# Two weights' low parts in the directed phase's second unit, a left copy ahead of the context, and the last phase's first values in the first two banks

## The chip, the cores and the metric

The kernel runs on one core of a Trainium2 chip. Its time is the device time of one execution in microseconds (us). The engines of the core that matter here are TensorE (PE, matmuls), VectorE (DVE), ScalarE (ACT) and GpSimd (POOL); SyncE (SP) issues the DMA transfers.

## The reference

128 graphs of 64 nodes with 384 features pass through four residual layers of attention kind. What is computed, cut down:

```python
h = jnp.maximum(_layernorm(x, axis=-1), 0.0)
x = x + _L0_gnn_ref(h, adj, ...)   # 12-head attention with an output projection
h = jnp.maximum(_layernorm(x, axis=-1), 0.0)
x = x + _L1_gnn_ref(h, adj, ...)   # two bilinear layers
h = jnp.maximum(_layernorm(x, axis=-1), 0.0)
x = x + _L2_gnn_ref(h, adj, ...)   # two directed layers, below
h = jnp.maximum(_layernorm(x, axis=-1), 0.0)
x = x + _L3_gnn_ref(h, adj, ...)   # 12-head attention, scores masked by adj

# a directed layer of _L2_gnn_ref
a = jax.nn.softmax(jnp.einsum('bid,bjd->bij', h, h) / temper, axis=-1)
delta = a * adjacency_matrix
attn = delta / (jnp.sum(delta, axis=-1, keepdims=True) + 1e-10)
hl, hs, hr = h @ wl.T + b_l, h @ ws.T + b_s, h @ wr.T + b_r
ctx = jnp.einsum('bij,bjd->bid', attn * upper, hl) + diag_a[..., None] * hs \
      + jnp.einsum('bij,bjd->bid', attn * lower, hr)
h = relu(layer_norm(ctx) * g + beta)
```

## The kernel before, in words

All 8192 rows are worked in 16 groups of 512 rows (four tiles of 128). The four layers are four phases of one program: l0, l1, l2 (the directed phase) and l3 (the last phase). Every engine has a stream of instructions written out by hand, in a fixed order; the streams meet only at semaphores.

An fp32 product is made of three passes: each operand is split into a high part (`w_hi`, `hT_hi`) and a low part (`w_lo`, `hT_lo`), and `split_matmul` (L58) adds high x high, high x low and low x high over three chunks of the features: nine matmuls into one of eight PSUM banks. The high part of a weight is a ScalarE copy, the low part a VectorE subtraction `raw - high` of 128x1152 elements (L2221 in the directed phase).

The directed phase has 32 units: a unit is one group in one of the two layers. Units 0 and 1 are groups 0 and 1 in layer 0; unit 2 is the first of layer 1. In a unit TensorE makes for each tile a left, a right and a self part (each one `split_matmul`), transposes the attention (L2512), weighs (context, L2567: two halves, tiles 0 and 1, then 2 and 3), passes on three transposes of the rows for the unit above (L2480) and its score products (L2501). VectorE copies each left part (L2293) and self part (L2302, L2306) out of PSUM with its bias, ScalarE each right part (L2164), to which GpSimd adds the bias (L2074). The parts share four banks, so part t+1 waits until the copy of an earlier part has been made: self part 2 waits for left copy 2 and for the contexts of tiles 0 and 1, left part 3 and right part 3 wait for self copies 0 and 1, self part 3 waits for left copy 3. VectorE makes the context (L2315), its statistics (L2323, L2327), the variance `l_c_var` (L2329); GpSimd takes the root of that (`l_c_scale`, L2079), and VectorE makes the shift `l_c_nb` (L2336) from it.

In the first unit (`below is None`), whose first parts are made in the phase's entry in other banks, VectorE's order after the variance is: left copy 2, two weights' low parts (`weights((CARRIED, CARRIED + 1))`), `passed(1)` (a low part of the rows, L2251), `l_c_nb`, left copy 3, `passed(2)`, self copy 2, self copy 3, and the third weight's low part. Those three weights are the ones of layer 1. TensorE waits for all three at the end of unit 1. SP loads the last phase's weights when all three are made.

The last phase's entry makes three query and three key products in banks 0 to 5, and the values of the first two tiles in banks 6 and 7. The scores go to banks 4 to 7, so they wait until VectorE has copied the queries (L640), ScalarE the keys (L442) and both values (L454). The later tiles' values go to banks 0 and 1.

Of the kernel before, what the change touches and what calls it, by code (L numbers as in the profile page):

```python
# [24 lines left out]
P = 128  # L25
GRAPHS, NODES, D = 128, 64, 384
# [5 lines left out]
HEADS, HD = 12, 32  # L32
# [4 lines left out]
CARRIED = 3  # L37
# [14 lines left out]
def split_matmul(nc, out, lhs, rhs, chunks=KC):  # L52

    n, last = 3 * chunks, None
    for c in range(chunks):
        for k, (a, b) in enumerate(((0, 0), (0, 1), (1, 0))):
            m = 3 * c + k
            last = nc.tensor.matmul(out, lhs[a](c), rhs[b](c), start=(m == 0), stop=(m == n - 1))  # L58
    return last
# [35 lines left out]
def attention_phase(nc, ctx, name, shared, x_in, adj_rows, x_out, biases, own_weights, next_weights):  # L95
# [112 lines left out]

    def k_sums(i, c):
        return banks[:, 2 * c + 1, :] if not proj and isinstance(i, int) and i == 0 else psW[k_bank[c]]  # L210

    def v_sums(i, t):
        return banks[:, 6 + t, :] if not proj and isinstance(i, int) and i == 0 and t < 2 else psW[v_bank[t]]

    q_bank, k_bank, v_bank = ((0, 0, 1), (1, 0, 0), (1, 1, 1, 0)) if proj else ((0, 0, 0), (1, 1, 1), (0, 1, 0, 1))

# [185 lines left out]
    def _(act):  # L402
# [46 lines left out]
        def values(i, t):  # L449
            act.wait_ge(v_done, i * TILES + t + 1)  # L450
            for g in range(2):
                for b in range(2):
                    src = v_sums(i, t)[NODES * g:NODES * (g + 1), 0:D].rearrange("p (a b d) -> p a b d", b=2, d=HD)
                    ins = nc.scalar.activation(vX[NODES * b:NODES * (b + 1), t, g, :, 0:HD], src[:, :, b, :], ACT.Copy)  # L454
            ins.then_inc(v_set, 1)

# [121 lines left out]
    def _(dve):  # L578
# [91 lines left out]
        def values(i, t):  # L670
            dve.wait_ge(v_done, i * TILES + t + 1)
            for g in range(2):
                for b in range(2):
                    part = slice(NODES * b, NODES * (b + 1))
                    src = v_sums(i, t)[NODES * g:NODES * (g + 1), 0:D].rearrange("p (a b d) -> p a b d", b=2, d=HD)
                    bias = bv[part, :].rearrange("p (a b d) -> p a b d", b=2, d=HD)[:, :, b, :]
                    ins = nc.vector.tensor_tensor(vX[part, t, g, :, 0:HD], src[:, :, b, :], bias, ALU.add)  # L677
            ins.then_inc(v_set, 1)
# [146 lines left out]
    def _(pe):  # L825
# [11 lines left out]
        def w_cols(s, cols):  # L837
            slot = s if proj else slot_of(s)
            return tuple((lambda c, w=w: w[:, slot, c, cols]) for w in (w_hi, w_lo))

        def h_cols(cols):
            return tuple((lambda c, x=x: x[:, c, cols]) for x in (hT_hi, hT_lo))
# [206 lines left out]
        if proj:  # L1049
            for t in range(TILES):  # L1050
                if t >= 2:
                    pe.wait_ge(hT_set, t - 1)
                transposes(0, t)
            pe.wait_ge(hT_set, TILES)
            pe.wait_ge(w_lo_set, Q + 1)
            queries(0, 0)
            pe.wait_ge(w_lo_set, K + 1)
            keys(0, 0)
            pe.wait_ge(q_set, 1)
            queries(0, 1)  # L1060
            pe.wait_ge(k_set, 1)
            queries(0, 2)
            pe.wait_ge(q_set, 2)
            keys(0, 1)
            pe.wait_ge(w_lo_set, n_w)
            pe.wait_ge(q_set, 3)
            values(0, 0)
            pe.wait_ge(k_set, 2)
            keys(0, 2)
            pe.wait_ge(v_set, 1)  # L1070
            values(0, 1)
            pe.wait_ge(zeroed, 2)
            wait_apart(k_set, 3)
            scores(0, 0)
            scores(0, 1)
            transposes(1, 0)
            transposes(1, 1)
            turns(pe, projected_turn)
        else:
            ended = shared["l2_ended"]  # L1080
            h_all = h_cols(slice(0, COLS))

            def first_product(bank, s, c, signal):
                split_matmul(nc, banks[:, bank, :], w_cols(s, slice(c * P, (c + 1) * P)), h_all).then_inc(signal, 1)

            def first_values(t):
                split_matmul(nc, banks[:, 6 + t, 0:D], h_cols(slice(t * P, (t + 1) * P)), w_cols(V, slice(0, D)))\
                    .then_inc(v_done, 1)

            pe.wait_ge(*ended["hT_set"])  # L1090
            pe.wait_ge(*ended["left_set"])
            pe.wait_ge(*ended["w_lo_set"])
            first_product(0, Q, 0, q_done)
            pe.wait_ge(*ended["right_read"])
            first_product(1, K, 0, k_done)
            pe.wait_ge(*ended["s_set"])
            first_product(2, Q, 1, q_done)
            pe.wait_ge(*ended["self_set"])
            first_product(3, K, 1, k_done)
            first_product(4, Q, 2, q_done)  # L1100
            pe.wait_ge(*ended["hT_hi_set"])
            first_product(5, K, 2, k_done)
            pe.wait_ge(*ended["c_set"])
            first_values(0)
            first_values(1)
            pe.wait_ge(zeroed, 2)
            pe.wait_ge(q_set, KC)
            pe.wait_ge(v_set, 2)
            wait_apart(k_set, KC)
            scores(0, 0)  # L1110
            scores(0, 1)
            turns(pe, plain_turn)
# [706 lines left out]
def directed_phase(nc, ctx, shared, x_in, adj, x_out, a, next_weights):  # L1819
# [394 lines left out]
    def _(dve):  # L2214
# [134 lines left out]
        def result(u, x):  # L2349
            if x == 0:  # L2350
                dve.wait_ge(xr_in, (u.q + 1) * 16)
            dve.wait_ge(affine_set, 2 * (u.q * TILES + x + 1))
            nc.vector.scalar_tensor_tensor(xr[:, x, :], out_rows[:, x, :], 0.0, xr[:, x, :], ALU.max, ALU.add)\
              .then_inc(y_set, 1)

        def unit(u, below, above, stats):
            carries = is_last(above)
            before = Unit(u.n - 2, u.q - 1, 1, 0) if finishes(u) else below if is_last(u) else None

            def passed(c):  # L2360
                hT_part(above.n * KC + c, above.parity, c)

            if below is not None:
                context(below, 2)
                context(below, 3)
            less_maximum(u)
            if below is not None:
                context_variance(below, 1)
            if below is None:
                left_copy(u, 0)  # L2370
                left_copy(u, 1)
            attention(u)
            if below is None:
                self_copy(u, 0)
                self_copy(u, 1)
            else:
                left_copy(u, 0)
            row_sums(u)
            if below is not None:
                context_norm(below, 1)  # L2380
                left_copy(u, 1)
            row_factors(u)
            attention_sides(u)
            if stats:
                q, g, x = to_normalise(u)
                if is_last(u):
                    dve.wait_ge(x1_in, 16)
                else:
                    dve.wait_ge(xl_in, q * 16)
                statistics(x)  # L2390
            if before is not None:
                result(before, 0)
                result(before, 1)
            if below is not None:
                self_copy(u, 0)
            row_diagonal(u)
            if stats:
                variances(g)
            passed(0)
            if below is not None:  # L2400
                self_copy(u, 1)
            if before is not None:
                result(before, 2)
                result(before, 3)
            if stats:
                shifts(q, g)
            step.catch_up()
            context(u, 0)
            context(u, 1)
            context_variance(u, 0)  # L2410
            left_copy(u, 2)
            if below is None:
                weights((CARRIED, CARRIED + 1))
            passed(1)
            context_norm(u, 0)
            if carries:
                next_weight(0)
            left_copy(u, 3)
            passed(2)
            if carries:  # L2420
                next_weight(1)
            self_copy(u, 2)
            if carries:
                next_weight(2)
            self_copy(u, 3)
            if below is None:
                weights((CARRIED + 2,))
            if is_last(u):
                context(u, 2)
                context(u, 3)  # L2430
                context_variance(u, 1)
                context_norm(u, 1)
                result(u, 0)
                result(u, 1)
                own_affine(3)
                result(u, 2)
                own_result(3)
# [329 lines left out]
```

## Time and profile before

| | us |
|---|---|
| median of three runs | 2691.43 |
| the three runs | 2688.78, 2691.43, 2691.6 |
| the profiled execution | 2689.87 |
| its span | 2688.1 |
| TensorE busy | 2649.9 (99%) |
| VectorE busy | 1775.0 (66%) |
| ScalarE busy | 1242.2 (46%) |
| GpSimd busy | 1070.2 (40%) |

The span is the time between the first and the last instruction of the profiled execution. In a timeline a bracket behind a row gives the idle time of the engine ahead of it and what ended it. The directed phase runs from about 1397 us to 2217 us of the span, and the last phase to the end.

### The profile page before, as it was taken

What the parts mean: (1) busy time and instruction counts of PE and PEld (TensorE: products, weight loads), DVE (VectorE), ACT (ScalarE), POOL (GpSimd) and SP (SyncE); (2) the same over time, 40 slices, a digit from 0 to 9 for tenths busy, and PEclk for the clock granted to TensorE, in tenths of its full rate; (3) what the DMA queues carried; (4) which work ended last, traced back from release to release, by engine and by line L of the source; (5) the groups of instructions that cost most, each with busy time, mean ns of one, the idle gap of its engine ahead of it and who ended that gap; (6) DMA issues with size and microseconds to landing.
All of it is one profiled execution on the core that took longest, in us unless ns stands there. A gap on an engine that the chain in (4) does not pass through costs nothing.

```text
span 2688.1 us, 78153 instructions
## 1 busy us (share of the span) xinstructions
PE 2649.9 (99%) x31118; PEld 2315.3 (86%) x31118; DVE 1775.0 (66%) x4024; ACT 1242.2 (46%) x2179; POOL 1070.2 (40%) x1094
## 2 busy tenths in 40 slices
PE   7999999999999999999999999999999999999998
PEld 6888888887888888888888888888888888998997
DVE  6777778775555555555577777777777785666664
ACT  4444444444453444444453433443343345655654
POOL 2433334442322322432333434434434454555454
PEclk9999999999999999999999999999999999999999
DMA  4222222225112212212221112112112122322321
GB/s 146 76 74 63 59 63 74 74 71 161 37 55 83 72 35 70 82 36 60 76 59 57 42 45 70 41 45 70 41 39 76 40 70 83 97 74 89 97 74 62
DMA packets 187155, 183.93 MB, mean 68 GB/s; under 512 B 79632, under 2 KB 186896, under 8 KB 187024
## 3 DMA queue, kind: packets, MB, share of 16 engines
q1 hardware_dynamic: 187024, 181.99, 22.1%
q8 instruction: 106, 1.74, 0.3%
q14 instruction: 25, 0.20, 0.0%
HBM read 131.61 MB, written 50.33 MB: 68 GB/s over the span
## 4 chain that ended last, share of the span: by engine, by line
PE 92%; DVE 4%; issue 2%; ACT 1%; SPq 0%; POOL 0%; DMA 0%; DVEq 0%; POOLq 0%; ACTq 0%
PE banks L58 68%; PE banks L2567 3%; PE banks L890 3%; PE banks L877 3%; PE banks L870 3%; PE banks L1750 2%; PE banks L2480 2%; PE banks L2501 2%; PE banks L1774 2%; PE banks L847 2%; PE banks L1710 1%; PE banks L899 1%; DVE l_o_rows L694 1%; DVE l_stats L598 1%; DVE l_vX L677 1%
## 5 line engine op out<-in xcount | busy, mean ns | idle before, releaser
L58 PE MATMUL banks<-w_hi,hT_hi 128*128 128x384 f32 x1152 | 401.0, 348 | 4.6 <-DVE l_left L2293 4.6
L58 PE MATMUL banks<-w_hi,hT_lo 128*128 128x384 f32 x1152 | 387.4, 336 | 0.0
L58 PE MATMUL banks<-w_lo,hT_hi 128*128 128x384 f32 x1152 | 386.5, 335 | 0.0
L58 PE MATMUL banks<-hT_hi,w_hi 128*128 128x512 f32 (+1 forms) x954 | 365.7, 383 | 1.2 <-DVE hT_lo L635 1.2
L58 PE MATMUL banks<-hT_hi,w_lo 128*128 128x512 f32 (+1 forms) x954 | 355.1, 372 | 0.0
L58 PE MATMUL banks<-hT_lo,w_hi 128*128 128x512 f32 (+1 forms) x954 | 354.5, 372 | 0.0
L1424 ACT ACTIVATE l_m<-banks 128x512 f32<-128x512 f32 x192 | 114.8, 599 | 399.6 <-PE banks L58 394.7
L336 POOL TENSOR_TENSOR l_s_d<-l_s_b,l_mx 128x768 f32<-128x768 f32 x128 | 188.8, 1475 | 206.9 <-DVE l_mx L665 191.5
L58 PE MATMUL banks<-w_hi,l_hT_hi 128*128 128x384 f32 x768 | 266.0, 346 | 0.8 <-DVE l_lin L1540 0.8
L58 PE MATMUL banks<-w_hi,l_hT_lo 128*128 128x384 f32 x768 | 258.4, 336 | 0.0
L58 PE MATMUL banks<-w_lo,l_hT_hi 128*128 128x384 f32 x768 | 258.2, 336 | 0.0
L58 PEld LDWEIGHTS banks<-w_hi,hT_hi 128*128 128x128 f32 x1152 | 217.0, 188 | 10.4 <-issue 3.8
L1349 POOL TENSOR_TENSOR l_c_root<-l_c_mv,l_half 128x2 f32<-128x2 f32 x64 | 44.7, 699 | 435.4 <-DVE l_c_mv L1557 435.4
L58 PEld LDWEIGHTS banks<-w_lo,hT_hi 128*128 128x128 f32 x1152 | 217.4, 189 | 0.7
L58 PEld LDWEIGHTS banks<-w_hi,hT_lo 128*128 128x128 f32 x1152 | 216.8, 188 | 0.0
L58 PEld LDWEIGHTS banks<-hT_hi,w_hi 128*128 128x128 f32 x954 | 180.4, 189 | 41.0 <-issue 9.6
L58 PEld LDWEIGHTS banks<-hT_hi,w_lo 128*128 128x128 f32 x954 | 180.1, 189 | 32.1
L58 PEld LDWEIGHTS banks<-hT_lo,w_hi 128*128 128x128 f32 x954 | 180.6, 189 | 26.7
L2079 POOL TENSOR_TENSOR l_c_scale<-l_c_var,l_half 128x2 f32<-128x2 f32 x64 | 48.6, 759 | 323.5 <-DVE l_c_var L2329 323.5
L459 ACT ACTIVATE l_eT<-banks 128x768 f32<-128x768 f32 x128 | 104.3, 815 | 143.7 <-PE banks L877 142.1
L58 PEld LDWEIGHTS banks<-w_hi,l_hT_hi 128*128 128x128 f32 x768 | 144.4, 188 | 4.6 <-DVE l_lin L1540 1.1
L350 POOL TENSOR_TENSOR xr<-xr,l_y_rows 128x384 f32<-128x384 f32 x60 | 62.0, 1033 | 209.1 <-ACT l_y_rows L473 209.1
(230 smaller groups left out, 6178.8 us busy)
## 6 DMA issues: line engine op xcount, KB each, us to landing
after_l<-xr SPq DMA_DIRECT2D x160, 192.0 KB, 1.9
l_xl<-after_l SPq DMA_DIRECT2D x37, 768.0 KB, 5.0
xr<-after_l SPq DMA_DIRECT2D x24, 768.0 KB, 4.6
xr<-in_x SPq DMA_DIRECT2D x64, 192.0 KB, 2.4
xr<-after_l SPq DMA_DIRECT2D x64, 192.0 KB, 2.3
out_x<-xr SPq DMA_DIRECT2D x64, 192.0 KB, 2.1
xa<-in_x SPq DMA_DIRECT2D x15, 768.0 KB, 5.2
xa<-after_l SPq DMA_DIRECT2D x11, 768.0 KB, 6.9
```

Source lines behind the costliest of these rows:

```text
L58: last = nc.tensor.matmul(out, lhs[a](c), rhs[b](c), start=(m == 0), stop=(m == n - 1))
L336: nc.gpsimd.tensor_tensor(s_d[:], s_b[:, t], mx[:, t, :].rearrange("p (h n) -> p h n", n=1).broadcast_to([P, HEADS, NODES]), ALU.subtract) ...
L350: nc.gpsimd.tensor_tensor(xr[:, t, :], xr[:, t, :], y_rows[:, t % 2, :], ALU.add).then_inc(y_set, 1)
L459: nc.scalar.activation(eT[:, t % 2].rearrange("p a n -> p (a n)"), P_all, ACT.Copy).then_inc(eT_set, 1)
L847: ins = nc.tensor.transpose(hT_sums(i, t)[:, c * P:(c + 1) * P], h[:, t, c * P:(c + 1) * P], ident[:])
L870: ins = nc.tensor.matmul(psS[NODES * g:NODES * (g + 1), r, lo + c * NODES:lo + (c + 1) * NODES], qT[head, c, nodes], kT[head, c, nodes], s ...
L877: ins = nc.tensor.transpose(P_all[:, a * P:(a + 1) * P], e_x[:, a * P:(a + 1) * P], ident[:])
L890: ins = nc.tensor.matmul(psS[NODES * g:NODES * (g + 1), r, lo:lo + HD + 1], eT[keys_b, x, a, NODES * g:NODES * (g + 1)], vX[keys_b, 2 * p ...
L1424: nc.scalar.activation(m[:, j % KC, :, 1 - j // KC, :], m_sums(i, k, j).rearrange("p (g n) -> p g n", n=NODES), ACT.Copy).then_inc(m_set, 1)
L1750: ins = nc.tensor.matmul(psU[first:first + HALF, t * P + cols.start:t * P + cols.stop], hT_whole[k % 2][:, c, t * P + first:t * P + first ...
L1774: ins = nc.tensor.matmul(psC[NODES * c:NODES * (c + 1), PAIR * p + b, 0:D + 1], delta[NODES * b:NODES * (b + 1), PAIR * p + c, :], lin[NOD ...
L2567: ins = nc.tensor.matmul(psC[NODES * c:NODES * (c + 1), odd, 0:D], dT[nodes, t, s, :], side[nodes, t, :], start=(s == 0), stop=(s == 1))
```

## The change

In the directed phase VectorE makes two of the three low parts in unit 1 instead of unit 0, one ahead of self copy 0 and one behind self copy 1. In unit 0, left copy 2 goes ahead of the contexts of tiles 0 and 1; in all other units it stays. In the last phase's entry the first two tiles' values go to banks 0 and 1, behind the first query and key copies, and the scores no longer wait for the value copies.

```diff
-    def v_sums(i, t):
-        return banks[:, 6 + t, :] if not proj and isinstance(i, int) and i == 0 and t < 2 else psW[v_bank[t]]
...
             def first_values(t):
-                split_matmul(nc, banks[:, 6 + t, 0:D], h_cols(slice(t * P, (t + 1) * P)), w_cols(V, slice(0, D)))\
+                split_matmul(nc, banks[:, t, 0:D], h_cols(slice(t * P, (t + 1) * P)), w_cols(V, slice(0, D)))\
                     .then_inc(v_done, 1)
...
-            pe.wait_ge(*ended["c_set"])
+            pe.wait_ge(q_set, 1)
             first_values(0)
+            pe.wait_ge(k_set, 1)
             first_values(1)
             pe.wait_ge(zeroed, 2)
+            pe.wait_ge(*ended["c_set"])
             pe.wait_ge(q_set, KC)
-            pe.wait_ge(v_set, 2)
             wait_apart(k_set, KC)
...
+        def is_second(u):
+
+            return isinstance(u.n, int) and u.n == 1
+
...
+            if is_second(u):
+                weights((CARRIED,))
             if below is not None:
                 self_copy(u, 0)
             row_diagonal(u)
...
                 result(before, 3)
+            if is_second(u):
+                weights((CARRIED + 1,))
             if stats:
                 shifts(q, g)
+            if below is None:
+                left_copy(u, 2)
             step.catch_up()
             context(u, 0)
             context(u, 1)
             context_variance(u, 0)
-            left_copy(u, 2)
-            if below is None:
-                weights((CARRIED, CARRIED + 1))
+            if below is not None:
+                left_copy(u, 2)
             passed(1)
```

The two readers of `v_sums` (the value copies of ScalarE and VectorE) read `psW[v_bank[t]]` instead.

## Rows read from the trace of the kernel before

**Rows 1.** The page's busy times: engine, busy us, share of the span, instructions.

```profile
PE 2649.9 (99%) x31118; PEld 2315.3 (86%) x31118; DVE 1775.0 (66%) x4024; ACT 1242.2 (46%) x2179; POOL 1070.2 (40%) x1094
```

**Rows 2.** TensorE's waits: who waited for whom, us in total, times, longest.

```profile
PE banks L847 <- ACT l_h L422: 7.8, 1, 7.8
PE banks L58 <- DVE l_left L2293: 4.6, 2, 3.5
```

**Rows 3.** TensorE's timeline, first unit: start, us, engine, line, operation [idle before].

```profile
1409.33 0.34 PE L58 MATMUL banks<-w_hi,hT_lo 128*128 128x384 f32 x1
1410.70 0.44 PE L58 MATMUL banks<-w_hi,hT_hi 128*128 128x384 f32 x1 [1.04 <-DVE l_left L2293]
```

**Rows 4.** The chain of waits, first and second unit: start, us, what.

```profile
1416.08 2.40 PE banks L58 x9
1418.48 2.45 PE banks L2567 x16
...
1433.02 1.45 PE banks L2567 x16
...
1440.18 4.68 PE banks L58 x27
```

**Rows 5.** Stretches: busy time of each engine, then TensorE's granted clock, DMA share, GB/s.

```profile
1416.00:1418.00 2.00, 1.92 (x9) 1.92 (x9) 1.00 (x2) 1.87 (x3) 0.00 (x0) 0.77 0.01 2
1418.00:1420.00 2.00, 2.00 (x14) 0.80 (x16) 1.43 (x3) 0.00 (x0) 0.00 (x0) 0.50 0.00 0
1420.00:1422.00 2.00, 2.00 (x46) 1.14 (x40) 1.97 (x3) 0.00 (x0) 0.00 (x0) 0.88 0.00 0
...
2224.00:2226.00 2.00, 0.41 (x17) 0.18 (x23) 0.00 (x0) 1.38 (x5) 0.00 (x0) 1.00 0.31 98
```

**Rows 6.** VectorE's timeline in the first unit.

```profile
1405.40 0.68 DVE L2251 TENSOR_TENSOR l_hT_lo<-hT_whole,l_hT_hi 128x512 fp32r<-128x512 f32 x1
1407.64 1.14 DVE L2315 SCALAR_TENSOR_TENSOR l_con<-l_selves,l_own,banks 128x384 f32<-128x384 f32 x2 [1.56 <-issue]
...
1410.02 0.16 DVE L2329 SCALAR_TENSOR_TENSOR l_c_var<-l_squared,l_c_mv 128x2 f32<-128x2 f32 x1
...
1410.57 3.43 DVE L2221 TENSOR_TENSOR w_lo<-w_raw,w_hi 128x1152 fp32r<-128x1152 f32 x2
1413.92 1.48 DVE L2251 TENSOR_TENSOR l_hT_lo<-hT_whole,l_hT_hi 128x512 fp32r<-128x512 f32 x1
...
1415.39 0.54 DVE L2293 TENSOR_TENSOR l_left<-banks,l_biases 128x384 f32<-128x384 f32 x1
...
1419.68 1.36 DVE L2221 TENSOR_TENSOR w_lo<-w_raw,w_hi 128x1152 fp32r<-128x1152 f32 x1
```

**Rows 7.** GpSimd's timeline in the first and second unit.

```profile
1410.26 0.71 POOL L2079 TENSOR_TENSOR l_c_scale<-l_c_var,l_half 128x2 f32<-128x2 f32 x1 [7.34 <-DVE l_c_var L2329]
1410.94 3.91 POOL L2074 TENSOR_TENSOR l_right<-l_right,l_biases 128x384 f32<-128x384 f32 x2
...
1438.78 1.07 POOL L2074 TENSOR_TENSOR l_right<-l_right,l_biases 128x384 f32<-128x384 f32 x1
```

**Rows 8.** VectorE's timeline in the second unit.

```profile
1427.40 0.56 DVE L2293 TENSOR_TENSOR l_left<-banks,l_biases 128x384 f32<-128x384 f32 x1 [0.92 <-PE banks L58]
...
1438.89 0.98 DVE L2336 SCALAR_TENSOR_TENSOR l_c_nb<-l_c_mv,l_c_scale 128x2 f32<-128x2 f32 x1
1439.79 0.55 DVE L2293 TENSOR_TENSOR l_left<-banks,l_biases 128x384 f32<-128x384 f32 x1
```

**Rows 9.** The chain of waits at the last phase's entry, ahead of the first scores.

```profile
2224.27 1.59 issue
```

**Rows 10.** ScalarE's timeline at the last phase's entry.

```profile
2221.16 0.69 ACT L442 ACTIVATE l_kT<-banks,l_bk 128x512 f32<-128x512 f32 x1 [3.00 <-PE banks L58]
2222.74 1.34 ACT L454 ACTIVATE l_vX<-banks 64x192 f32<-64x192 f32 x4 [0.90 <-PE banks L58]
2224.30 1.34 ACT L454 ACTIVATE l_vX<-banks 64x192 f32<-64x192 f32 x4 [0.22 <-PE banks L58]
```

More of the change, by code:

```diff
@@ L452, in values @@
                 for b in range(2):
-                    src = v_sums(i, t)[NODES * g:NODES * (g + 1), 0:D].rearrange("p (a b d) -> p a b d", b=2, d=HD)
+                    src = psW[v_bank[t]][NODES * g:NODES * (g + 1), 0:D].rearrange("p (a b d) -> p a b d", b=2, d=HD)
                     ins = nc.scalar.activation(vX[NODES * b:NODES * (b + 1), t, g, :, 0:HD], src[:, :, b, :], ACT.Copy)
@@ L674, in values @@
                     part = slice(NODES * b, NODES * (b + 1))
-                    src = v_sums(i, t)[NODES * g:NODES * (g + 1), 0:D].rearrange("p (a b d) -> p a b d", b=2, d=HD)
+                    src = psW[v_bank[t]][NODES * g:NODES * (g + 1), 0:D].rearrange("p (a b d) -> p a b d", b=2, d=HD)
                     bias = bv[part, :].rearrange("p (a b d) -> p a b d", b=2, d=HD)[:, :, b, :]
```

## The prediction

> **What bounds the kernel now.** I read the page's busy times first, then TensorE's waits, then the chain of waits around the two edited places, then the timelines of VectorE, GpSimd and ScalarE there. TensorE is busy 99% of the span [rows 1], so the rest of the program is a row of matmuls that nothing holds up, and only a stall of TensorE, or matmuls at the slower clock, can give time back. The waits of TensorE are 14 rows that add up to 31.7 us; the largest is the start of the program (7.8), the second is the one that the change aims at: 4.6 us in two waits for VectorE's `l_left`, the longer of 3.5 [rows 2]. Whatever is gained at such a place is kept to the end, because TensorE runs nearly without a break behind it.
>
> The two waits lie in the directed phase's first unit. The other stall that the change touches is in the last phase's entry, where the chain shows 1.59 us of "issue" before the first scores [rows 9].
>
> **First unit, before.** TensorE's right part 3 issues its last matmul at 1409.33; matmuls of this kind follow each other every 0.17 us (1.56 for nine, below), so self part 2 could start at 1409.50; it starts at 1410.70 [rows 3]: it waits for left copy 2, which VectorE makes at 1410.10 only because it stands behind the context and its variance. Self part 3 could then follow at once, and starts at 1416.08 [rows 4], because left copy 3 (1415.39 to 1415.93) stands behind two low parts of weights (3.43), `l_hT_lo` (1.48) and the small `l_c_nb`, which ends as the copy begins [rows 6]. Behind the idle time TensorE's granted clock is 0.77, 0.50 and 0.88 in three stretches of 2 us from 1416 [rows 5], that is, the 1.2 GHz level for a part of them. The nine matmuls of self part 3 take 2.40 there against 1.56 (a third of 4.68 for 27), the context 2.45 against 1.45 in the next unit [rows 4]: 0.84 + 1.00 = 1.84 us that the stall costs on top of itself.
>
> **The change, part by part.**
>
> *Left copy 2 sooner.* It moves in front of the context. Its matmuls have long ended; VectorE is free from 1406.08 (1405.40 + 0.68) until the context at 1407.64, 1.56 us in which the trace shows it idle [rows 6], and the copy takes 0.55 [rows 8]. So it costs nothing, left copy 2 is done by 1406.7, and self part 2 starts at 1409.50. Were the gap not there, the context would come 0.55 later and self part 2, which also waits for that context (done 1408.78), would find it done at 1409.33, still in time.
>
> *Two low parts leave the first unit.* Left copy 3 now waits for: the variance (1410.18), `l_hT_lo`, GpSimd's `l_c_scale` (1410.26 to 1410.97), `l_c_nb` [rows 6, 7]. What is late next is `l_c_nb`. With nothing in its way it would run at once and left copy 3 would end near 1411.64; TensorE resumes 0.15 later (1415.93 to 1416.08), at 1411.79. But GpSimd starts its next addition on `l_right` at 1410.94, and in the second unit the same pair is seen: `l_right` from 1438.78 for 1.07, and `l_c_nb` at 1438.89 takes 0.98 where `l_c_var`, of the same form, takes 0.16 in rows 6, ending with GpSimd's instruction [rows 7, 8]. I take this case, the nearest row: `l_c_nb` ends near 1411.96, left copy 3 is seen from 1411.88 to 1412.43, TensorE resumes at 1412.58. That is 3.50 sooner than 1416.08; a stall of 1.5 us stays in front of self part 3, which could start at 1411.07 (1409.50 + 1.57). The bounds are 1411.79 (a gain of 4.3) and 1412.58 plus 0.8, if `l_hT_lo` is stretched as it was to 1.48 (2.7).
>
> The Trainium skill, page GPSIMD Engine Reference, section 1 (Specifications), says that GpSimd's SBUF interfaces are shared with VectorE and contend with VectorE instructions with two SBUF inputs; `l_c_nb` is one, the left copy (one input in PSUM) is not. The trace agrees with the 0.98 us of `l_c_nb` ending beside `l_right`. By that rule the stall in front of self part 3 stays 1.5 us, by an uncontended price it would be 0.7: this is the rule that speaks against the change, and it costs 0.8 us of the gain.
>
> *The clock.* A stall of 1.59 us at 2224.27 is followed by a granted clock of 1.00 [rows 5, 9]. So I take the 1.84 us back in full; if the clock falls in spite of the shorter stall, none of it.
>
> *The same low parts in the second unit.* Each instruction is 128x1152; the one that ran alone took 1.36 [rows 6], two 2.72. The pair in the first unit took 3.43 beside GpSimd's two additions that took 3.91; less 1.36 that leaves 2.07 for the other. The first goes ahead of self copy 0, the second behind self copy 1, and from there all copies come 2.72 later. The work that hides this is TensorE's: left part 3, right part 3 and self part 2. Self part 3 starts at 1440.18 + 2 x 1.56 = 1443.30 [rows 4]; left copy 3 ends at 1440.34 [rows 8] and has to be there 0.15 ahead, so there are 2.81 us of room against 2.72. It just fits: I take 0. With one of the two at 2.07 the stall is 0.6; with both, 1.3. VectorE may also enter the unit some 0.6 us behind TensorE's pace (an estimate from 1.36 of third low part, now at full clock right before the first unit's last contexts); its 0.92 us of idle time before left copy 1 takes that up [rows 8]. The third low part costs nothing more than before. Both ScalarE high parts stay where they were. TensorE's own wait for the low parts stands at the unit's end, behind self part 3. On SP's queue the three loads of the last phase's weights wait for all low parts and so go out later in the stream; the load behind them on that queue waits for the third unit's attention anyway.
>
> *Last phase, first values in banks 0 and 1.* TensorE now waits for the first query and key copies before these matmuls, which are its seventh and eighth products: ScalarE's last key copy (the third) starts at 2221.16 [rows 10], so the first copies are past by then and the added waits cost nothing. The scores lose the wait for both value copies. ScalarE's copies run 2222.74 to 2224.08 and 2224.30 to 2225.64, and the scores started 0.2 behind the second; the last matmul of the values hands over at 2224.27, so the scores start at once: 1.59 gone [rows 9, 10], less 0.04 for the hand-over, 1.55. The other condition, the third key copy, ends at 2221.85. What is late next: the values of tile 2 write bank 0 again and need the first copy (2224.08), two us later than that; the two value copies still run on ScalarE, beside the scores and the next transposes, and ScalarE's next work is now due 1.55 sooner. The chain scores, VectorE, GpSimd, ScalarE moves as a whole. Bounds: 1.59, and 0.8 if half is given back there because ScalarE is still at the second copy.
>
> **The sum.** 3.50 + 1.84 + 0 + 1.55 = 6.9 us. The profiled execution took 2689.87 (span 2688.1 and 1.77 around it): 2683.0. The runs before are 2688.78, 2691.43 and 2691.6; with the profiled one their mean is 2690.4, less 6.9 is 2683.5, which I give. From the median of 2691.43 it would be 2684.5.
>
> **Rivals.**
> *Uncontended.* `l_c_nb` slips in before GpSimd's addition: 0.8 more, 2682.7. For it: both are released by the same instruction. Against: in the second unit GpSimd was first.
> *The clock still falls* in the first unit, or the second unit stalls as at its bounds (0.6 to 1.3): 1.3 to 1.84 less, 2684.8 to 2685.4; both together 2686.6. For it: 2.81 of room against 2.72 is thin. Against: of GpSimd's additions none stands in the trace where the low parts will be.
> *The change does not do what it says* in one place: left copy 3 is held by something else in the first unit and only the last phase's part works: 2690.4 - 1.55 - 1.2 = 2687.6. Against: the rows show nothing else in its queue.
> *Slower.* The second unit becomes bound by VectorE: each low part costs 2.07 and waits for a GpSimd addition of 1.07 besides, so 2 x 3.14 = 6.3 on the queue, 3.5 over the room; a stall that long brings the clock down as at 1416, and what is left of the unit (3.1 of matmuls, 1.45 and 1.55) takes twice as long, 6.1 more. That is 9.6 lost against 6.9 won: 2693.1. It decides when the low parts together take over 6 us. No row shows such a price.
>
> **How the numbers follow.** Forecast 0.58, uncontended 0.10, the clock or a stall in the second unit 0.22, not done 0.07, slower 0.03. The likeliest gives 2683.5. The range has to take in the bounds of the price of `l_c_nb` (0.8 down), a second-unit stall with the clock's 1.84 (to 2686.6), and the spread of the runs before (2.8 us over four): 2680.2 to 2687.8. About 5.4 us (0.2%) is what can be told from no change here. The forecast clears that by 1.5 us; I count three tenths of the clock-or-stall case and nearly all of the first two: 0.76 faster. Within 0.2%: 0.21. Slower: 0.03.
>
> **What would show it.** After: no wait before self part 2; before self part 3 a wait of about 1.5 us for `l_left`, with `l_c_nb` of about 1 us ending beside `l_right`; granted clock 1.00 up to the second unit; the context there 1.45; unit 2's first matmul 5.3 sooner; two low parts in the second unit at about 1.36 each and no wait of TensorE in that unit over 0.3; in the last phase 0 instead of 1.59 before the scores. It is wrong if the clock's row is still below 1 after the first unit, if TensorE waits for `l_left` in the second, or if the gain at the scores is missing from the next chain.

## The result, and the profile after

The changed kernel takes 2683.71 us (median of 10 runs, 2681.36 to 2687.03) against 2691.7 for the kernel before (10 runs, 2688.78 to 2694.52); the ratio is 0.9972 with the interval 0.9964 to 0.9981, that is 7.5 us less (5.1 to 9.7; the two medians themselves lie 8.0 apart). The forecast was 2683.5. In two later comparisons, each with new runs of both kernels, it was 2684.94 and 2684.28, ratio 0.9976 both times (0.9966 to 0.9985 and 0.9967 to 0.9985).

The page's busy times answer to [rows 1]: TensorE makes the same 31118 matmuls in 5.1 us less of busy time. Of this, 1.9 lies in the first unit, where fewer of them run at the slower clock and one of two waits is gone; the rest lies in stages whose code is the same (in two later traces of the changed kernel it is busy for 2648.9 and 2648.4).

```profile
PE 2644.8 (99%) x31118; PEld 2312.0 (86%) x31118; DVE 1775.1 (66%) x4024; ACT 1241.2 (46%) x2179; POOL 1068.9 (40%) x1094
```

TensorE's waits, for [rows 2]: of the two for left copies (4.6 us) one is left.

```profile
PE banks L58 <- DVE l_left L2291: 1.7, 1, 1.7
PE banks L58 <- DVE l_lin L1538: 1.1, 1, 1.1
```

TensorE's timeline in the first unit, for [rows 3]: this is the only row there with idle time ahead of it. It is self part 3; self part 2 follows right part 3 without a gap.

```profile
1412.57 0.41 PE L58 MATMUL banks<-w_hi,hT_hi 128*128 128x384 f32 x1 [1.73 <-DVE l_left L2291]
```

The chain of waits, for [rows 4]: self part 3 took 2.40 and the context 2.45, they take 1.83 and 1.45. The 1.83 is 0.27 more than the 1.56 of nine such matmuls without a wait ahead of them; below this is called the restart. In the second unit 27 matmuls take 4.68 as before.

```profile
1412.57 1.83 PE banks L58 x9
1414.39 1.45 PE banks L2574 x16
1415.85 1.55 PE banks L2508 x48
...
1427.94 1.45 PE banks L2574 x16
...
1435.10 4.68 PE banks L58 x27
```

Stretches with the granted clock behind TensorE's busy times and the other engines', for [rows 5]: it stays at 1.00, the 2.4 GHz level.

```profile
1410.00:1414.00 4.00, 2.27 (x13) 1.98 (x12) 3.31 (x5) 2.01 (x3) 2.89 (x3) 1.00 0.94 288
1414.00:1418.00 4.00, 4.00 (x71) 2.75 (x70) 3.49 (x5) 0.35 (x1) 0.00 (x0) 1.00 0.15 36
```

VectorE in the first unit, for [rows 6]: left copy 2 stands in the gap, which shrinks from 1.56 to 1.09; then `l_c_nb`, 0.95 long, and left copy 3.

```profile
1405.61 0.55 DVE L2291 TENSOR_TENSOR l_left<-banks,l_biases 128x384 f32<-128x384 f32 x1
1407.25 1.14 DVE L2313 SCALAR_TENSOR_TENSOR l_con<-l_selves,l_own,banks 128x384 f32<-128x384 f32 x2 [1.09 <-issue]
...
1409.72 0.69 DVE L2249 TENSOR_TENSOR l_hT_lo<-hT_whole,l_hT_hi 128x512 fp32r<-128x512 f32 x1
1411.01 0.95 DVE L2334 SCALAR_TENSOR_TENSOR l_c_nb<-l_c_mv,l_c_scale 128x2 f32<-128x2 f32 x1 [0.60 <-POOL l_c_scale L2077]
1411.88 0.55 DVE L2291 TENSOR_TENSOR l_left<-banks,l_biases 128x384 f32<-128x384 f32 x1
```

GpSimd, for [rows 7]: the root takes 1.09 beside VectorE's `l_hT_lo`, where it took 0.71 beside left copy 2; the two additions 1.94, not 3.91, now that no low part of a weight runs beside them.

```profile
1409.88 1.09 POOL L2077 TENSOR_TENSOR l_c_scale<-l_c_var,l_half 128x2 f32<-128x2 f32 x1 [7.34 <-DVE l_c_var L2327]
1410.95 1.94 POOL L2072 TENSOR_TENSOR l_right<-l_right,l_biases 128x384 f32<-128x384 f32 x2
```

VectorE in the second unit, for [rows 8]: the two low parts at 1.34 and 1.36, left copy 3 at the end. It is done at 1437.82, and TensorE's self part 3 starts at 1435.10 + 2 x 1.56 = 1438.22, with no idle time.

```profile
1426.82 1.34 DVE L2219 TENSOR_TENSOR w_lo<-w_raw,w_hi 128x1152 fp32r<-128x1152 f32 x1
...
1431.36 1.36 DVE L2219 TENSOR_TENSOR w_lo<-w_raw,w_hi 128x1152 fp32r<-128x1152 f32 x1
...
1437.27 0.55 DVE L2291 TENSOR_TENSOR l_left<-banks,l_biases 128x384 f32<-128x384 f32 x1
```

The chain at the last phase's entry, for [rows 9]: the 72 matmuls of the products are followed by the scores at once. ScalarE still makes the second value copy beside them, for [rows 10].

```profile
2203.55 15.64 PE banks L58 x72
2219.19 1.22 PE banks L867 x72
```

```profile
2219.22 1.34 ACT L451 ACTIVATE l_vX<-banks 64x192 f32<-64x192 f32 x4 [0.22 <-PE banks L58]
```

**Stage by stage.** TensorE's instructions are the same in all these kernels and in the same order, so a stage can be cut at the same instruction in every trace. The table gives the time from the start of one such instruction to the start of the next, from TensorE's first matmul to its last; the boundaries are named by their time in the trace of before. A turn is one group's work in a phase.

```
                      start   60 to  620 to  700 to  first  second  rest of  entry of  turns 2   last
                      to 60    620     700    1397   unit   unit    directed last ph.  and on    turn
before                52.36  559.91   79.93  697.19  25.22  25.65   760.49    39.92    407.96   26.49
after                 51.94  559.94   80.31  697.19  20.51  25.67   760.49    38.30    407.99   24.68
after, second trace   54.09  559.94   83.81  697.21  20.52  25.67   760.49    38.28    408.00   24.55
after, third trace    53.74  560.75   83.63  697.18  20.49  25.67   760.49    38.30    407.94   24.35
directed_only         53.03  559.81   84.17  697.18  20.49  25.67   760.49    39.96    407.98   26.76
last_only             52.77  559.85   79.71  697.18  25.19  25.66   760.49    38.30    407.98   27.62
low_back              50.97  560.01   80.34  697.19  25.23  25.66   760.49    38.28    408.04   23.84
one_back              52.97  559.94   84.05  697.20  21.15  25.67   760.49    38.30    407.97   24.95
extra_low             51.57  559.86   83.40  697.18  20.51  26.91   760.49    38.30    407.96   24.95
both_left             52.22  559.87   83.51  697.19  19.76  25.67   760.49    38.30    407.98   26.49
right_first           54.03  560.17   83.07  697.20  18.52  25.81   760.49    38.30    408.06   24.95
right_first_2         54.14  560.03   83.55  697.20  18.52  25.82   760.49    38.28    407.98   27.17
```

Two columns changed by the edit: the first unit by 4.7 us and the last phase's entry by 1.6, together 6.3. They repeat to 0.1 us, as do the long stages behind 700. The other 2.2 of the 8.5 us by which the two profiled spans differ (2688.1 and 2679.6) lie in stages whose code is the same (0.4 of it ahead of the first matmul), and which move by up to 4.5 us from one execution to the next.

### The profile page after: what moved, and what is told of

Its sections match the earlier page's. It is cut to its first block, busy times and chain, and to the rows that moved or that the text cites. A ratio compares the mean times of both kernels' runs of the same rounds, so it can differ in the third digit from the quotient of the medians.

```text
span 2679.6 us, 78153 instructions
## 1 busy us (share of the span) xinstructions
PE 2644.8 (99%) x31118; PEld 2312.0 (86%) x31118; DVE 1775.1 (66%) x4024; ACT 1241.2 (46%) x2179; POOL 1068.9 (40%) x1094
## 4 chain that ended last, share of the span: by engine, by line
PE 94%; DVE 3%; issue 1%; ACT 1%; SPq 0%; DMA 0%; POOL 0%; DVEq 0%; POOLq 0%; ACTq 0%
PE banks L58 69%; PE banks L2574 3%; PE banks L887 3%; PE banks L874 3%; PE banks L867 3%; PE banks L1748 2%; PE banks L2487 2%; PE banks L2508 2%; PE banks L1772 2%; PE banks L844 2%; PE banks L1708 1%; PE banks L896 1%; PE banks L2519 0%; DVE l_o_rows L691 0%; DVE l_vX L674 0%
```

## The experiments

The theory: the two low parts of weights stood in left copy 3's way and cost the first unit a stall and then the clock; in the second unit TensorE's work covers them; and the value copies held the scores up. The rival for the first unit: left copy 2, or luck between two profiles, has a share of its own.

**after_again and after_third**, the changed kernel once more.

> The changed kernel once more, for its spread beside the parts. Theory (stall, clock and last phase's wait each give their share): 2684 +- 3, 7 to 8 us under the kernel before on the same chip; stage by stage again: first two directed units 4.7 shorter, last phase's entry 1.6 shorter, the stages between unchanged within 0.1. Rival (part of the 8.5 us between the two profiles was luck, above all the 1.8 us in the last turn and the 0.4 ahead of the directed phase): these two go away or turn round in this trace, and the two places keep their 6.3.

> The changed kernel beside the one with GpSimd's additions first, for a comparison on the same chip: 2684 to 2685, first unit 20.5 us, second 25.7, last phase's entry 38.3, as in its two traces so far.

Measured: 2684.94 (9 runs) and 2684.28 (11 runs), against 2691.71 and 2689.93 before. The two places keep their 4.7 and 1.6. What lies ahead of the directed phase turned round (the first four stages together are 5.7 and 5.9 us longer than before's), so the 0.4 there was luck. The last turn is about 2 us shorter in both again, but its code is the same, and in directed_only, last_only and right_first_2 it takes 26.76, 27.62 and 27.17, so none of it is the change's. What differs there is TensorE's granted clock: in that turn it is 1.00 in low_back (23.84 us), 0.96 to 0.98 in the three traces of the changed kernel, 0.88 in before and 0.83 in directed_only, while TensorE's idle time there is 4.5 to 4.6 us in ten of the twelve traces (5.9 in last_only and right_first_2). Why the clock differs is open.

**directed_only and last_only**, one half of the change each. Their edits are the halves of the diff above.

> Only the directed phase's edits; the last phase's entry as before. Theory: first two units 4.7 shorter than before (stall 1.7 and not 1.0 + 3.5, granted clock 1.00 there), the entry of the last phase as before with its 1.59 of issue; 4.7 +- 1 us under before. Rival (the parts help each other, or the directed gain is given back later): less than 3.5 us under before.

> Only the last phase's edit; the directed phase as before. Theory: 1.55 to 1.6 us between the end of the entry's products and the scores gone, everything behind it as much sooner, both stalls in the directed phase's first unit and the clock below 1 still there; 1.6 +- 1 us under before. Rival (the scores' chain gives it back): under 0.5 by the start of the last phase's second turn.

Measured: 2687.35 (11 runs; ratio 0.9982, 0.9973 to 0.9991, 4.8 us less) and 2689.45 (11 runs; 0.9991, 0.9982 to 1.0, 2.4 us less, with no change just at the end of its interval). The stages give each half its own column and nothing else: 20.49 for the first unit in the one, 38.30 for the entry in the other. The two effects add, and neither is given back in the 408 us behind the entry. The chain of directed_only still has the issue of [rows 9]; that of last_only goes on without it:

```profile
2208.64 15.64 PE banks L58 x72
2224.28 1.58 issue
2225.86 1.28 PE banks L870 x66
```

```profile
2208.76 15.64 PE banks L58 x72
2224.39 1.23 PE banks L867 x72
```

**low_back**: both low parts in the first unit again, left copy 2 still early.

```diff
-            if is_second(u):
-                weights((CARRIED,))
...
-            if is_second(u):
-                weights((CARRIED + 1,))
...
             if below is not None:
                 left_copy(u, 2)
+            else:
+                weights((CARRIED, CARRIED + 1))
             passed(1)
```

> The changed kernel with both low parts back in the first unit, behind the variance; left copy 2 stays in front of the contexts. Theory (the low parts in left copy 3's way are the whole gain of the directed phase, left copy 2 alone moves the wait and not the time): no wait before self part 2, one of about 4.6 us before self part 3, the clock below 1 behind it, the first two units within 0.3 us of before; 4.4 to 4.9 us over the changed kernel. Rival (left copy 2 sooner brings its 1 us by itself): 3.5 to 3.9 over the changed kernel, the first two units 1.0 shorter than before.

Measured: 2689.98 (10 runs; 0.9994, 0.9984 to 1.0003). The first unit is 25.23, before's 25.22: left copy 2 alone brings nothing. The wait that it takes away comes back in front of self part 3: one of 4.37, where before had 1.04 and 3.52, and self part 3 and the context behind it take 5.35 instead of 4.85. Three views show it: TensorE's timeline, its stretch behind the wait, and the chain, where nine matmuls take 3.22 at the lower level (0.50, 1.2 GHz).

```profile
1414.53 0.66 PE L58 MATMUL banks<-w_hi,hT_hi 128*128 128x384 f32 x1 [4.37 <-DVE l_left L2291]
```

```profile
1416.00:1418.00 2.00, 2.00 (x10) 1.54 (x12) 0.21 (x1) 0.31 (x1) 0.00 (x0) 0.50 0.00 0
```

```profile
1414.53 3.22 PE banks L58 x9
1417.75 2.13 PE banks L2572 x16
```

**one_back**: one of the two low parts in the first unit again (`weights((CARRIED,))` in the place shown above).

> The changed kernel with one of the two low parts (the first) back in the first unit. Theory (the clock's loss depends on the length of the stall, 1.7 kept it and 3.5 behind 1.0 lost it): the low part takes 1.4 to 2.1, the wait before self part 3 is 3.1 to 3.9 and the granted clock falls behind it, so that the first two units lose the wait's 1.4 to 2.1 and 1 to 1.6 of clock against the changed kernel. Rival (the clock fell before because of two stalls near each other): the clock stays at 1.00 and the loss is 1.4 to 2.1 alone.

Measured: 2687.42 (10 runs; 0.9981, 0.9972 to 0.9991). The sizes of both theories were off: the wait is 2.4 and not 3.1 or more, the clock stays at 1.00, and the first unit is 21.15, only 0.65 longer than after's, though the low part takes 1.35. VectorE's timeline tells why. It waited 0.60 for the root before `l_c_nb` in the changed kernel; here the low part fills that time. GpSimd's root, begun beside the low part, takes 1.75 and is done when `l_hT_lo` ends.

```profile
1418.36 0.41 PE L58 MATMUL banks<-w_hi,hT_hi 128*128 128x384 f32 x1 [2.39 <-DVE l_left L2291]
```

```profile
1414.85 1.35 DVE L2219 TENSOR_TENSOR w_lo<-w_raw,w_hi 128x1152 fp32r<-128x1152 f32 x1
1416.12 0.68 DVE L2249 TENSOR_TENSOR l_hT_lo<-hT_whole,l_hT_hi 128x512 fp32r<-128x512 f32 x1
1416.80 0.95 DVE L2334 SCALAR_TENSOR_TENSOR l_c_nb<-l_c_mv,l_c_scale 128x2 f32<-128x2 f32 x1
```

```profile
1415.01 1.75 POOL L2077 TENSOR_TENSOR l_c_scale<-l_c_var,l_half 128x2 f32<-128x2 f32 x1 [7.35 <-DVE l_c_var L2327]
```

So of the first unit's 4.7 us the first low part taken out (with the clock that came back) brought 4.1, the second 0.65. Whether it is a stall's length alone that brings the clock down, this run does not settle: stalls of 1.7 and 2.4 kept it, one of 4.4 lost it, and so did one of 3.5 that stood 1.8 behind another of 1.0.

**extra_low**: a third low part in the second unit.

```diff
             if is_second(u):
                 weights((CARRIED,))
+                nc.vector.tensor_tensor(w_lo[:, slot_of(CARRIED + 1)], raw[:, CARRIED + 1], w_hi[:, slot_of(CARRIED + 1)].bitcast(F32), ALU.subtract)
```

> The changed kernel with one more low part in the second unit: the second of the two is made a first time ahead of self copy 0, and then again in its place (same values). Theory (the cover in the second unit is 2.8 us, 2.7 of it used; left copy 3 there ends 0.25 before it would hold TensorE up): the 1.36 us more show as a wait of 1.0 to 1.2 for left copy 3 in the second unit, the clock stays at 1.00. Rival (VectorE has more slack there than the rows show): no wait, same time.

Measured: 2686.7 (9 runs; 0.9981, 0.9971 to 0.9991). The second unit is 26.91 against 25.67, 1.24 longer for 1.35 more of VectorE's work. The clock stays at 1.00. The waits are smaller than I said and they are two: 0.50 for left copy 2 and 0.23 for left copy 3, together 0.73 us; the third of the waits below is the first unit's 1.7. The rest, 0.5, is about two restarts. So the two low parts use up the second unit's cover but for 0.1 to 0.25 us (the latter is 1438.22 less 1437.82 and the 0.15 of a hand-over, from the rows of after).

```profile
PE banks L58 <- DVE l_left L2291: 2.5, 3, 1.7
```

```profile
1440.07 0.44 PE L58 MATMUL banks<-w_hi,l_hT_hi 128*128 128x384 f32 x1 [0.50 <-DVE l_left L2291]
...
1442.13 0.42 PE L58 MATMUL banks<-w_hi,l_hT_hi 128*128 128x384 f32 x1 [0.23 <-DVE l_left L2291]
```

**both_left**: left copy 3 also in front of the contexts.

```diff
             if below is None:
                 left_copy(u, 2)
+                left_copy(u, 3)
             step.catch_up()
...
-            left_copy(u, 3)
+            if below is not None:
+                left_copy(u, 3)
             passed(2)
```

> The changed kernel, and in the first unit left copy 3 as well in front of the contexts, behind left copy 2. Theory (what is left of the stall is l_c_nb held up by GpSimd's addition, in left copy 3's way): the copy fits into the 1.1 us in which VectorE waits for the context, TensorE has no wait before self part 3, and next it waits some 0.6 us for GpSimd's addition to l_right before the context: 1.3 to 1.5 us under the changed kernel. Rival (the rest of the first unit is set by GpSimd and the contexts, not by left copy 3): 0 to 0.3 us under the changed kernel.

Measured: 2685.26 (10 runs; 0.9976, 0.9966 to 0.9985), which the times can't tell from the changed kernel's 2684.94. The first unit is 19.76, 0.75 shorter, about halfway between what the theory and the rival said. The wait in front of self part 3 is gone as expected, and so is its 0.27 of restart, but the new wait for GpSimd is twice what I said. Both additions take 2.48 and not 1.94, since VectorE now goes from `l_c_nb` straight to `l_hT_lo`, which runs beside the second.

```profile
PE banks L2576 <- POOL l_right L2072: 1.2, 1, 1.2
```

```profile
1413.60 1.09 POOL L2077 TENSOR_TENSOR l_c_scale<-l_c_var,l_half 128x2 f32<-128x2 f32 x1 [7.34 <-DVE l_c_var L2327]
1414.67 2.48 POOL L2072 TENSOR_TENSOR l_right<-l_right,l_biases 128x384 f32<-128x384 f32 x2
```

**right_first**: that kernel, and GpSimd's additions for tiles 2 and 3 ahead of its root in the first unit.

```diff
+            if below is None:
+                right_bias(u, 2)
+                right_bias(u, 3)
             root(u, 0)
-            right_bias(u, 2)
-            right_bias(u, 3)
+            if below is not None:
+                right_bias(u, 2)
+                right_bias(u, 3)
```

> The kernel with both left copies in front of the contexts, and in the first unit GpSimd's additions to l_right of tiles 2 and 3 ahead of the root l_c_scale. Theory (with left copy 3 gone from behind l_c_nb the next wait is the context's for GpSimd's l_right, 1.2 us with both additions at 1.2 behind the root): no wait of TensorE in the first unit, 1.2 us less than with both left copies alone, 1.3 to 1.5 less than the changed kernel, if the second unit doesn't stall; VectorE enters it about 1.5 us late, which may give back up to 0.7. Rival (something else, the score products or the third low part, sets the start of the second unit): at most 0.3 less than the changed kernel.

> The same kernel as right_first, beside the changed one. Theory (its first unit is 2.0 us shorter than the changed kernel's and the rest the same): stages again 18.5, 25.8 and 38.3, median 1.9 +- 1.2 us under the changed kernel's of this call. Rival (the 2 us come back in the second unit or later): the same median within 0.5, and a second unit over 27.

Measured: 2681.84 (7 runs; 0.9964, 0.9952 to 0.9975), and beside the changed kernel on the same chip 2683.04 (10 runs; 0.9971, 0.9961 to 0.998) against 2684.28. By the stages it is 2.0 shorter in the first unit and 0.15 longer in the second, in both traces: a gain of 1.85 over the changed kernel that the medians (1.2) agree with but do not show beyond their spread. TensorE waits for nothing in the first unit. And `l_c_nb`, with no addition of GpSimd behind its root, is 0.16 long (the rows behind it are the addition and the root):

```profile
1417.31 0.16 DVE L2338 SCALAR_TENSOR_TENSOR l_c_nb<-l_c_mv,l_c_scale 128x2 f32<-128x2 f32 x1 [1.57 <-POOL l_c_scale L2077]
```

```profile
1415.22 1.39 POOL L2072 TENSOR_TENSOR l_right<-l_right,l_biases 128x384 f32<-128x384 f32 x1 [3.33 <-ACT l_right L2166]
1416.57 0.71 POOL L2077 TENSOR_TENSOR l_c_scale<-l_c_var,l_half 128x2 f32<-128x2 f32 x1
```

## Why the prediction was right

- *Left copy 2 costs nothing and self part 2 starts at once.* Right. The gap went from 1.56 to 1.09. What the prediction did not say is that this edit by itself is worth nothing (low_back), since self part 3 waits for left copy 3 in any case. Whether it is worth anything beside the moved low parts is not shown: no run moves them and leaves left copy 2 in its old place, and VectorE is idle for 0.60 us ahead of `l_c_nb` in the changed kernel, enough for a copy of 0.55.
- *TensorE resumes 3.50 sooner.* The mechanism was right, `l_c_nb` held up by GpSimd's addition: 0.95 in the changed kernel, 0.16 in right_first, where the addition is out of its way. The size was off by 0.4: I took the root at 0.71. That was its price beside left copy 2, with the low parts begun 0.31 after it [rows 6, 7]; with left copy 2 gone from there it ran beside `l_hT_lo` and took 1.09 (beside a low part it takes 1.75, in low_back and one_back). That the two engines hold each other up was in the prediction, but in the forecast it was applied to `l_c_nb` only; the bound of 2.7 for this term took a price of this kind in.
- *1.84 us of clock come back.* The clock stayed at 1.00 as forecast; the term was 0.27 too large, for nine matmuls that start after a wait take 1.83 (1.80 in one_back) and not 1.56, at the full clock. The trace of before had such a case and I did not use it: self part 2 behind its wait of 1.04 [rows 3], from 1410.70 to 1412.57. That the clock would stay was argued from one stall of 1.59, and the 1.7 was near it; in the same trace a stall of 3.10 ahead of 614.52 was followed by the slower clock (0.50 from 616 to 618), and the prediction did not weigh it. Together the first unit gave 4.7 and not 5.34.
- *The second unit covers both low parts.* Right, 25.67 against 25.65, and it was as thin as the 2.81 against 2.72 said: the room left is 0.1 to 0.25. The low parts took 1.34 and 1.36, the value of the one that ran alone.
- *The last phase's entry gives 1.55.* 1.62, kept to the end, with the same value in last_only. Nothing was given back on ScalarE.
- *The sum.* 6.9 forecast, 6.3 by the stages; the ratios say 7.5, 6.5 and 6.5 in three comparisons, with intervals that hold both. The forecast of 2683.5 lies 0.2 from the first median; that it is so near is luck of a few tenths either way, given runs that spread over 5.7 us.
- *The rivals.* Uncontended: refuted here by 0.95. It was less far off than "in the second unit GpSimd was first" says, for in the trace of before 13 of the 42 `l_c_nb` that began behind an addition on `l_right` took 0.15 (the last section has the rule). The clock or a stall in the second unit: refuted by 1.00 and 25.67. Not done in one place: refuted by directed_only; its 1.2 us, beside the 1.55, is a term for which no row was given and no run shows one. Slower: it needed low parts of over 6 us together, and they took 2.70.

## What to carry to other kernels

When an engine is 99% busy, look for the stalls one by one and ask of each what stands in the queue ahead of the copy that ends it; then, before moving work, subtract the new place's cover in the same way, for here it fitted with 0.1 to 0.25 us to spare. Moving one of two copies that gate successive steps moves the wait, not the time. And once the long wait is gone the next is set by a third engine: both left copies ahead of the contexts gave 0.75 us in the first unit, and GpSimd's order on top of them the rest of the 1.85; that order alone was not run.

## What the runs showed of the hardware

**VectorE and GpSimd hold each other up, to the end of an instruction, and hundredths of a microsecond decide which waits.** Over the twelve traces, `l_c_nb` (128x2) began 0.04 us or more behind the start of a GpSimd addition on `l_right` 356 times; each time it ended 0.01 to 0.03 us behind that addition, so that it took 0.78 to 0.99. It began at most 0.03 behind it 156 times, and each time it took 0.15. With nothing on GpSimd beside it, it took 0.15 or 0.16. A case of each kind from the trace of before is in [rows 7, 8] and here:

```profile
1578.87 0.15 DVE L2336 SCALAR_TENSOR_TENSOR l_c_nb<-l_c_mv,l_c_scale 128x2 f32<-128x2 f32 x1
```

```profile
1578.86 1.05 POOL L2074 TENSOR_TENSOR l_right<-l_right,l_biases 128x384 f32<-128x384 f32 x1
```

The other way, GpSimd's root took 1.09 beside `l_hT_lo`, 1.75 beside a low part and 0.71 behind `l_hT_lo` (right_first), its addition 1.39 beside `l_hT_lo` and 1.01 alone. The left and self copies out of PSUM, with one input in SBUF, took 0.53 to 0.56 throughout, 206 of the 320 in before beside an instruction of GpSimd. The Trainium skill, page GPSIMD Engine Reference, section 1 (Specifications), says that GpSimd shares its SBUF interfaces with VectorE and contends with VectorE instructions with two SBUF inputs. These runs agree with it on which instructions are held up; the sizes above are theirs alone.

**The spread between traces lies in three places, none of them in the change.** One is the stage 620 to 700, 79.7 to 80.3 us in four traces and 83.1 to 84.2 in the other eight. There the bilinear phase's first turn waits for rows that come by DMA. In the changed kernel's first trace TensorE waited 1.1 us for `l_lin` and the clock stayed; in the second 3.1, with the clock below 1 behind it:

```profile
PE banks L58 <- DVE l_lin L1538: 3.1, 1, 3.1
```

```profile
668.00:672.00 4.00, 4.00 (x16) 4.00 (x15) 0.98 (x2) 0.00 (x0) 0.00 (x0) 0.57 0.99 274
```

The statistics that wait for the transfer start at 655.31 and 659.79; 2.4 of these 4.5 us come from earlier stages, so it landed 2.1 later, and the stage is 3.5 longer. What makes it land later I did not try. The program's start (51.0 to 54.1) and its last turn (23.8 to 27.6) are the other two; in both TensorE has waits of 1 to 3 us, and the clock is below 1 for a part (in the last turn in all traces but low_back's, the shortest). A gain of 1 to 2 us is therefore plain in a stage cut at the same instruction and hardly visible in a median of ten runs.
